# Loading x through ACT's queue beside the first adjacency tiles on SP's queue, in a two-layer graph kernel on Trainium2

## The reference, cut to what matters

```python
# layer 0
h = jnp.maximum(_layernorm(x, axis=-1), 0.0)
x1 = swish((adj @ h) @ W0 + b0)
x = x + swish((adj @ x1) @ W0 + b0)
# layer 1
h = jnp.maximum(_layernorm(x, axis=-1), 0.0)
a_hat = adj + eye
a_norm = a_hat * d[:, None] * d[None, :]      # d = rowsum(a_hat) ** -0.5
x = x + (a_norm @ h) @ W1.T + b1
```

## Time and profile before

| | us |
|---|---|
| median of three executions | 1447.98 |
| lowest, highest | 1447.57, 1449.35 |
| profiled execution: its own time | 1447.59 |
| profiled execution: span of its instructions | 1444.3 |
| PE busy | 1384.3 |
| DVE busy | 1011.0 |
| ACT busy | 684.1 |

### The profile page before, as it was taken

The page is one execution under the profiler, slowest core; times in us unless marked ns, Lnnn a source line. Parts: engine busy times, 40 slices in busy tenths (PEclk is TensorE's granted clock), DMA queues, the critical chain, the costliest instruction groups (busy, mean ns, idle before and its releaser), DMA issues.

```text
span 1444.3 us, 18282 instructions
## 1 busy us (share of the span) xinstructions
PE 1384.3 (96%) x6598; PEld 649.9 (45%) x6598; DVE 1011.0 (70%) x2316; ACT 684.1 (47%) x781; POOL 34.1 (2%) x30
## 2 busy tenths in 40 slices
PE   2878999999999999999999999999999999999998
PEld 0333444444444444444444454454444444444444
DVE  7788888999988786776774777877665555545331
ACT  6878878887777657656560112222311221132000
POOL 1100000000000000000000011101000000000000
PEclk9999999999999999999999999999999999999999
DMA  9989999999999888887760112111433233333000
GB/s 378 383 356 415 410 412 418 409 397 404 392 381 389 322 351 319 332 350 277 300 267 30 37 52 66 66 52 63 178 125 146 110 132 137 133 118 123 23 15 24
DMA packets 56111, 335.49 MB, mean 232 GB/s; under 512 B 6224, under 2 KB 6736, under 8 KB 18256
## 3 DMA queue, kind: packets, MB, share of 16 engines
q1 hardware_dynamic: 48960, 322.20, 56.7%
q10 hardware_dynamic: 7056, 12.06, 2.2%
HBM read 322.44 MB, written 11.80 MB: 231 GB/s over the span
## 4 chain that ended last, share of the span: by engine, by line
PE 79%; DMA 9%; DVE 7%; issue 3%; ACT 2%; DVEq 0%; ACTq 0%; SPq 0%
PE acc_ps L589 21%; PE acc_ps L590 21%; PE acc_ps L530 9%; PE acc_ps L531 9%; DMA ring<-adj 9%; PE early_ps L500 6%; PE early_ps L499 6%; PE z_ps L482 3%; PE kept_ps L508 2%; PE kept_ps L509 2%; DVE marks L846 1%; ACT marks L665 1%; DVE stats L825 1%; DVE ring L342 0%; ACT unused L710 0%
## 5 line engine op out<-in xcount | busy, mean ns | idle before, releaser
L710 ACT ACTIVATE unused<-ring 128x2048 uint8<-128x2048 uint32 x220 | 420.0, 1909 | 91.2 <-DMA ring<-adj 81.0
L530 PE MATMUL acc_ps<-marks,node_a 128*128 128x512 fp8e4 x1024 | 392.8, 384 | 52.3 <-DVE node_a L839 30.3
L531 PE MATMUL acc_ps<-marks,node_a 128*128 128x512 fp8e4 x1024 | 392.4, 383 | 1.8 <-issue 1.8
L590 PE MATMUL acc_ps<-ring,node_a 128*128 128x512 fp8e4 x1024 | 388.1, 379 | 0.0
L589 PE MATMUL acc_ps<-ring,node_a 128*128 128x512 fp8e4 x1024 | 388.1, 379 | 0.0
L846 DVE TENSOR_SCALAR marks<-ring 128x2048 uint8<-128x2048 f32 x226 | 277.1, 1226 | 67.6 <-DMA ring<-adj 38.8
L342 DVE TENSOR_SCALAR ring<-bits 128x256 uint32<-128x256 uint32 (+1 forms) x784 | 159.7, 282 | 89.0 <-PE acc_ps L590 88.7
L530 PEld LDWEIGHTS acc_ps<-marks,node_a 128*128 128x128 f16 x1024 | 101.0, 99 | 186.8 <-issue 71.9
L751 ACT ACTIVATE nT<-acc_ps 128x512 f32<-128x512 f32 x16 | 9.6, 597 | 313.3 <-PE acc_ps L590 313.3
L499 PE MATMUL early_ps<-marks,node_b 128*128 128x512 fp8e4 x416 | 157.7, 379 | 0.0
L500 PE MATMUL early_ps<-marks,node_b 128*128 128x512 fp8e5 x416 | 157.7, 379 | 0.0
(11 more groups left out here) (117 smaller groups left out, 1106.1 us busy)
## 6 DMA issues: line engine op xcount, KB each, us to landing
ring<-adj SPq DMA_DIRECT2D x256, 1024.0 KB, 7.6
marks<-adj SPq DMA_DIRECT2D x36, 1024.0 KB, 5.0
xch<-x SPq DMA_DIRECT2D x16, 256.0 KB, 2.7
xn_scratch<-xnew ACTq DMA_DIRECT2D x16, 256.0 KB, 2.0
xch<-xn_scratch SPq DMA_DIRECT2D x16, 256.0 KB, 2.8
out<-xnew ACTq DMA_DIRECT2D x16, 256.0 KB, 2.0
part_scratch<-stage ACTq DMA_DIRECT2D x13, 256.0 KB, 5.4
marks<-part_scratch SPq DMA_DIRECT2D x13, 256.0 KB, 3.0
```

The lines of the kernel that those rows point to most:

```text
L530: nc.tensor.matmul(acc_ps[c % 2][:, :], hi_of(node_a16, j), byte, start=(j == 0), stop=False)
L531: last = nc.tensor.matmul(acc_ps[c % 2][:, :], lo_of(node_a16, j), byte, start=False, stop=(j == NB - 1))
L590: last = nc.tensor.matmul(into[:, :], lo_of(node, j), byte.bitcast(low), start=False, stop=closes)
L710: nc.scalar.activation(unused[:, :], slot(g).bitcast(U32), ACT.Sign, accum_out=nz_count[:, g:g + 1]).then_inc(counted, 1)
```

## The change

Before, SP's queue holds x's first part (1 MB), tile 0, x's second part (1 MB), tile 1, x's third part (2 MB), tile 2, tile 3. ACT's queue holds the four small loads (64 KB each). After, SP's queue holds x's first part and tiles 0, 1, 2, 3, and ACT's queue holds x's second part, its third part, and then the four small loads. Nothing else differs.

```diff
             load_x(0, NORM_PARTS[0], x_in[0])
-            load_tile(0)
-            load_x(NORM_PARTS[0], NORM_PARTS[1], x_in[1])
-            load_tile(1)
-            load_x(NORM_PARTS[0] + NORM_PARTS[1], NORM_PARTS[2], x_in[2])
-            load_tile(2)
-            load_tile(3)
+            for g in range(RING):
+                load_tile(g)
             for g in range(RING, NC * TC):
...
         @block.scalar
         def _(act):
+            for part in range(1, len(NORM_PARTS)):
+                a, n = sum(NORM_PARTS[:part]), NORM_PARTS[part]
+                act.dma_start(b3(node_b[:, a * D:(a + n) * D]), x_v[:, a:a + n, :]).then_inc(x_in[part], 16)
             act.dma_start(w_sb[:, 0:D], w0).then_inc(w_in, 16)
```

## The result

Over the executions timed side by side, the changed kernel took 1451.23 us (median of 12) and the kernel before 1447.89 us: a ratio of 1.0022, with a 95% interval of 1.0014 to 1.0029. So the change costs 2 to 3.3 us; 1450.0 had been forecast. The profiled execution took 1450.69 us, 3.1 us more than that of before, with a span of 1447.1 (before: 1444.3).

A forecast was written before the change was run, and what follows sets the result against it. Tile arrivals were taken to set the end until 232 us, then PE alone. Tile 10, through DVE's mark(6), makes the stream 2.4 us late: 1447.6 + 2.4 = 1450.0 us, range 1446.8 to 1452.2.

The forecast's parts named there:

- Steps 1 and 3: Loads at the start: sharing engines packet by packet, x's first part lands 2.3 us later at 8.2, tile 0 at 15.6.
- The rival of longer turns: DMA queues at the start: a queue keeps an engine for 8 packets, so no loss, 1447.6 us; chance 0.08.
- Steps 2 and 4: DVE from first_norm(0) to mark(6): 2.4 us late both ways, by its own work and by ACT and POOL.
- Step 3: ACT behind tile 0: make_h(2) begins at 29.1 instead of 27.50, so tile 9's issue is also 1.6 us late.
- Step 5: Tile 10: issued at 42.5, lands at 47.3, 2.4 us later; DVE's lateness then falls to ACT's 1.6 us.
- the hand-over: Marks at 227.83, matmul at 232.35 us: before it tile arrivals set the end, behind it PE alone.
- Step 6: Small loads behind 3 MB: last lands at about 28 us, PE starts 5 us later, at no cost.
- lost cover: PE's idle 6.26 us until 37.99 hides its late start; without it PE is late by what exceeds 31.4 us.
- The sum: Whole kernel: the tile stream 2.4 us late at 47 us reaches the end, 1447.6 + 2.4 = 1450.0 us.
- the second hole: DMA nearly idle at 78 to 81 us (share 0.02), after tile 19's landing and DVE work; moves along unchanged.
- The slower rival: Path over ACT and POOL to mark(6): 1.4 us more from a late tile 0 and one meeting, 1451.4 us; chance 0.27.
- The delay is made up: Tile stream: up to 2.1 of the 2.4 us come back if slow packets aren't the tiles' own, 1447.9 us; chance 0.15.

The follow-up runs named there:

- big_beside: Kernel before with x's third part (2 MB, 16 KB packets) loaded through ACT's queue ahead of the small loads: 1451.73 against 1448.44 us, ratio 1.0026.
- tile0_first: Kernel before with tile 0 ahead of x's first part on SP's one queue: ratio 1.0000, median 0.55 us later.
- order: Kernel before with ACT marking tiles 4 and 5 ahead of make_h(2) and make_h(3), DVE marking tile 6 right behind first_norm(2): 1448.56 against 1447.75 us, 1.0004.
- act_late: Kernel before with one extra ACT operation, an unused mark of tile 3, ahead of act_mark(3): 1450.50 against 1447.75 us, ratio 1.0022.
- split_x2: Changed kernel with x's third part loaded as two 1 MB DMAs (8 KB packets) on ACT's queue: 1449.62 against 1447.75 us, ratio 1.0015.
- split_again: Changed kernel with x's third part as two 1 MB DMAs on ACT's queue, run a second time: 1449.31 against 1448.10 us, ratio 1.0007.
- the second trace: The changed kernel run once more, unaltered: 1450.49 against 1448.44 us for the kernel before, ratio 1.0012.
- before_again: The kernel before, run once more unaltered as a measure of chance: ratio 1.0000, span 1.0 us longer.
- x_waits: Changed kernel with ACT issuing x's second and third part only when the first has landed: 1448.43 against 1448.44 us, ratio 1.0000.

## Why the prediction was right, and where it wasn't

The kernel was forecast 2.4 us slower; medians say 3.3 and 2.05, the two profiled executions 3.1 and 2.5. That the number held is in part luck: the sum has nothing outside the span, where 0.6 us came (medians), and nothing for the 0.6 us of the stream that came back.

- **Steps 1 and 3, the two landings.** x's first part at 8.2 (measured 8.05), tile 0 at 15.6 (15.4). The turns of one packet are shown three times: by 24 and 24 packets before the change, by 48 and 52 after it, and by the landing at 10.7 us in big_beside. The rival of longer turns falls. The Trainium skill, page "DMA: Bandwidth & Descriptors", section "Queues, rings and completion order", says 9 to 17 descriptors in a turn; these traces show one 8 KB or 16 KB packet.
- **Steps 2 and 4, DVE.** 2.4 us late at `mark(6)`; measured 2.3. But the lateness was not the same "both ways": by its own work DVE was 1.25 us late at `h_low(0)`, because two short operations that had met POOL (0.9 to 1.0 us each) became one, and the wait of 0.94 us for POOL brought the rest. So about 1 us of DVE's lateness came from tile 0 through ACT, not from x's first part. Step 3 had ACT 1.6 us late at `make_h(2)`; measured 1.3.
- **Step 5 is where the reasoning failed, though its number held.** It named tile 10, and with it `mark(6)`, as the point that decides, and said that lost transfer time doesn't come back. Tile 10 was 2.2 us late as forecast, but by tile 19 only 1.6 us were left, in both traces. tile0_first (DVE late, ACT on time) gave no loss that can be measured, order (DVE 4.3 us early) no gain, and act_late (ACT late, `mark(6)` on time) gave the whole loss. So at the end ACT's lateness costs more than DVE's; the intervals of act_late and tile0_first don't overlap. How is not shown. ACT is busy without a gap from 27 to 57 us, but it doesn't hold up the stream there: the DMA engines are busy throughout. The 0.6 us came back because tile 13 landed 3.4 us behind tile 12 in the kernel before and 2.5 us behind it in the changed one, with the engines busy in both. Nor can the two be split cleanly: tile 10 was 1.5 us late in tile0_first and 1.4 in act_late, and split_x2 and split_again had ACT on time and still lost 1.9 and 1.2 us, 1.2 and 0.4 of it in the span.
- **The rest of the loss.** Between tile 19 (1.6 us) and the hand-over (2.8) the profiled execution lost another 1.2 us; the second trace lost less. before_again drifts by 0.6 us over the same stretch, and by 1.0 up to the end, with nothing changed. I take this as chance and have not shown it.
- **Step 6, the small loads.** They landed at 27.6 us (forecast 28), at no cost. But the price that I gave for a lost cover, what exceeds 31.4 us, is wrong: in x_waits PE began at 34.7 and the end did not move. PE is not what the stream waits for until 230 us, and it makes up more than its first idle time. The forecast of 4 us of idle DMA between 25 and 45 us was off too: there were 2.6.
- **The sum and the rivals.** That a microsecond of the stream before 230 us is one at the end held for the change and for the second hole, where 3.4 us less of idle DMA between 75 and 84 us gave 2.5 at the end. The slower rival, a longer path over ACT and POOL, did not come: `mark(6)` began at 41.10, at the forecast place. "The delay is made up" was right in part: 0.6 of 2.2 us came back, by faster transfers, as it said. But one row that it rests on was misread: the 293 GB/s of 9 to 12 us go with a share of 0.80, so they are no 293 at full work but 293 / 0.80 = 366.

## What to carry to other kernels

A load that everything waits for should have the DMA engines to itself: a load on another queue does not run beside it but takes every other turn, and with larger packets more than half of the bytes. If a second queue is to carry later data, let it wait for the first load's semaphore, as in x_waits, where the cost was gone. And before pricing a late start by the buffer it delays first, look at what each engine behind it does: here 1.7 us of lateness on ACT, which works without a gap, cost 2.5 us of span, and 1.6 us on DVE, which has gaps, nothing that could be measured. When kernels differ by a few microseconds, compare spans as well as times: 0.6 us of this change lie outside the span.

## What the runs showed of the hardware that was not expected

The engines moved fewer bytes while the small loads were in flight. In the kernel before that was 293 GB/s from 9 to 12 us, at a share of 0.80: a fifth of the engines' time was idle although the next loads had been issued. In the changed kernel, where the small loads land between 18 and 28 us, it was 308 GB/s at a full share from 21 to 24, in the row above, with 404 where it had been 293. Whether the small loads cause it was not tried. Turns of an 8 KB packet (0.31 us) and a 512 B one (0.027 us) on 16 engines would leave some 413 GB/s, an estimate from the packet times in the prediction.

A 1 MB load issued into an empty queue landed after 4.8 us in both kernels, of which 2.5 us are transfer. From this I estimate that a slot which is freed more than about 2.3 us before the queue runs dry costs nothing, and that every microsecond later is idle time of the engines. In the rows of 47 to 69 us each next tile was issued earlier than that, and the engines had no idle time.
